# A query and key projection as three rounded products, with the context tile split by ScalarE and GpSimd

## The chip, the cores and the metric

The kernel runs on one NeuronCore of a Trainium2 chip. The metric is the device time of one execution in microseconds (us). The engines are TensorE (PE in the profile; PEld is its loading of weights), VectorE (DVE), ScalarE (ACT), GpSimd (POOL) and SyncE (SP, which here only issues transfers).

## The reference, cut to what matters

Thirty-two tiles of 128x1024 pass through four layers with a residual each: a first cross-attention, a feed-forward with signed weights, a second cross-attention and a mixture of low-rank products. The change is in the first one, with `init` the context tile:

```
q = einsum('dc,bct->btd', Wq, init) + bq          # Wq, Wk: 64 x 128, init: 128 x 1024
k = einsum('dc,bct->bdt', Wk, init) + bk
attention = softmax(einsum('btd,bds->bts', q, k))
out = einsum('bts,bsc->bct', attention, einsum('oc,bct->bto', Wv, x) + bv)
```

Everything is float32. TensorE multiplies either full float32 operands or operands rounded to a shorter form (`F32R`). Where the kernel wants nearly full accuracy at the rate of the rounded form, it splits each operand into a rounded part and a rest ("hi" and "lo") and adds three products: hi x hi, lo x hi and hi x lo.

## The kernel before

Each engine has a program written by hand, and semaphores tie them together. All five run the same loop over k (`iterations`, L633): two opening iterations, 30 in full form, two closing ones. Iteration k works on three tiles at once: it *prepares* tile b = k, *attends* with tile a = k - 1 and runs the *chain* (feed-forward, second attention, low-rank products) of tile c = k - 2. `nth(per, b, n)` is the count that a semaphore has when tile b has reached its n-th event. `half(h)` is columns 512h to 512h + 511.

The order on TensorE within one full iteration (`body`, L1195):

- eight `query_scores(a, t)` (L1141) into the two banks of `scores`, whose row maxima DVE takes (L880), with the products `keys_through_queries` (L1152 to L1155) and the first steps of the chain between them;
- the feed-forward (L1166, L1167), and `key_scores(a, s)` (L1180, L1181) for s = 0 and 1;
- a loop over s = 0 to 7: `key_scores(a, s + 2)`, then parts of the chain, then `weigh_values(a, s)` (L1192), six products that add attention times values to `acc`. `weigh_values` waits at its start for both `p_hi_ready` and `p_lo_ready` of its s;
- within s = 7 and ahead of `weigh_values(a, 7)`: the second attention's products (L1300, L1302), the query and key projection of the next tile, `wqkT` x `c_in` into `scores[0]` (L1307), column sums by `ones` (L1314), eight transposes of `c_in` (L1321), and two transposes of `den_wide` (L1325);
- after the loop: transposes of `xn_3` (L1345), the values of the next tile (L1127, called `values`), the low-rank products (L1357, L1370 to L1376). The next iteration's transposes of `xn_1` (L1207) wait for `out_ready`, which DVE's last step L1099 gives.

For each s, ACT writes `prob` as an exponential of the scores (L783) and the rounded `p_hi` (L790); DVE writes `p_lo = prob - p_hi` (L991) and from s = 1 on adds `prob` to `p_sum` (L996, L999). `prob`, `p_hi`, `p_lo` and `p_sum` are all in SBUF, so L991 and L999 read two SBUF operands. At s = 6 the DVE runs `p_lo` of 6, `p_sum` of 6, then `kwT` (L917) and a reciprocal (L1026), and at s = 7 `p_lo` of 7 (L991), `res` (L1031), statistics (L862 to L870) and the copy `den_wide` (L1038).

After the projection, ACT works without a pause through `q_hl` and `k_hh` (L812, L814, a half each), `cT_hi` (L819, L821), `xn_3` (L727, two halves) and `den_rows` (L733, two halves). DVE's L903, L904 (`x1_half`) wait for `den_rows`, and behind them on DVE stand all steps up to L1099.

GpSimd does little: `res = x1 + bias_rows` on 128x1024 once in an iteration (L705), and four times two operations on 128x1 (L696, L697, called `norm_scale`).

`oscale` is a 128x1024 tile that is also `xn_2` and `result`. `q_hl` holds the query of the tile that is attended; its last reader in an iteration is `key_scores(a, 7)`, at s = 5.

Of the kernel before, what the change touches and what calls it, by code (L numbers as in the profile page):

```python
# [18 lines left out]
F32 = mybir.dt.float32  # L19
# [29 lines left out]
def build(nc, x, ctx_, wq0, bq0, wk0, bk0, wv0, bv0, w_ffn, b_ffn, gate, ics, ocs,  # L49
# [13 lines left out]
    with top:  # L63
        def sb(name, shape, dt=F32, stack=top):
            return stack.enter_context(nc.sbuf_tensor(name, shape, dt))
# [5 lines left out]
        ident = sb("ident", [P, P])  # L71
        ones = sb("ones", [P, 32])
        minus_half = sb("minus_half", [P, 1])
        wqkT = sb("wqkT", [P, P])
        wvT = sb("wvT", [P, P])
        bqk_col = sb("bqk_col", [P, 1])
        bv_col = sb("bv_col", [P, 1])
# [45 lines left out]
        with ExitStack() as tmp:  # L123
# [65 lines left out]
            with nc.Block() as block:  # L189
# [85 lines left out]
                def _(dve):  # L275
# [45 lines left out]
                    for n, (kind, i) in enumerate(groups):  # L321
                        if kind == "sign":
                            continue
                        s = bank[n % 8]
                        dve.wait_ge(filled, n + 1)
                        if kind == "small":
                            nc.vector.tensor_copy(wqkT[:, :], s[:, 0:P])
                            last = nc.vector.tensor_copy(wvT[:, :], s[:, P:2 * P])
                        elif kind == "gate":
                            dve.wait_ge(fold_made, 6)  # L330
                            both = s[:, 0:T * 2 * E].rearrange("p (t e) -> p t e", t=T)
                            nc.vector.tensor_copy(gateT[:, :, 0:E], both[:, :, 0:E])
                            last = nc.vector.tensor_copy(lowT[:, :, HR:HR + E], both[:, :, E:2 * E])
                        elif kind == "low":
                            last = nc.vector.tensor_scalar(lowT[:, 4 * i:4 * i + 4, 0:HR],
                                                           s[:, :].rearrange("p (t e) -> p t e", t=4), LORA, None, ALU.mult)
                        elif kind == "b":
                            turned = s[:, :].rearrange("q (t p) -> q t p", t=4)
                            hi, lo = (b[:, :].rearrange("q (p t) -> q t p", t=T)[:, 4 * i:4 * i + 4, :] for b in (bT_hi, bT_lo))
                            nc.vector.tensor_copy(hi, turned).then_inc(b_hi_made, 1)  # L340
                            dve.wait_ge(b_hi_made, i + 1)
                            last = nc.vector.tensor_tensor(lo, turned, hi.bitcast(F32), ALU.subtract)
                        elif kind == "bk_col":
                            nc.vector.tensor_copy(key_bias[:, :], s[:, 0:T])
                            last = nc.vector.tensor_copy(bqbk[:, :], s[:, T:T + 1])
                        elif kind == "m":
                            dve.wait_ge(m_hi_made, i + 1)
                            if i >= STAGES:
                                dve.wait_ge(m_stored[i % STAGES], 16 * (i // STAGES))
                            last = nc.vector.tensor_tensor(m_stage[:, i % STAGES, :], s[:, :],  # L350
                                                           m_hi[:, f_order[i // 2], columns(i)].bitcast(F32), ALU.subtract)
                        else:
                            last = nc.vector.tensor_copy(query_bias[:, columns(i)], s[:, :])
                        last.then_inc(copied, 1)
# [129 lines left out]

        xnT = sb("xnT", [P, T, P])
        den_wide = xnT[:, 0:2, :].rearrange("p t c -> p (t c)")
        oscale = sb("oscale", [P, D])
        c_val = sb("c_val", [P, D])
        stat = [sb(f"stat{i}", [P, 12]) for i in range(4)]
        mean_var = [sb(f"mean_var{i}", [P, 2]) for i in range(4)]  # L490
# [17 lines left out]
        result = oscale  # L508
        attn = sb("attn", [P, P])
        gate_parts = attn  # L510
        attnT = sb("attnT", [P, P])
        low = attn
        lowT_hi = sb("lowT_hi", [P, P], F32R)
        lowT_lo = sb("lowT_lo", [P, P], F32R)

        def psum(name, shape):
            return top.enter_context(nc.psum_tensor(name, shape, F32))
# [15 lines left out]

        cT_done = sem("cT_done")
        qk_done = sem("qk_done")
        doubled = sem("doubled")
        v_done = sem("v_done")
        maxscores_done = sem("maxscores_done")
# [102 lines left out]
        with nc.Block() as block:  # L641
# [47 lines left out]
            @block.gpsimd  # L689
            def _(pool):  # L690
                def norm_scale(i, b):

                    pool.wait_ge(var_ready[i], nth(1, b, 1))
                    pool.wait_ge(normed[i], nth(2, b - 1, 2) if i == 3 else nth(1, b - 1, 1))
                    pool_norm[i].begin(b)
                    pool_norm[i].chain(pool, nc.gpsimd.tensor_tensor(rstd[i][:, :], var_eps[i][:, :], minus_half[:, :], ALU.pow))  # L696
                    nc.gpsimd.tensor_tensor(shift[i][:, :], neg_mean[i][:, :], rstd[i][:, :], ALU.mult).then_inc(shift_ready[i], 1)  # L697
                    pool_norm[i].end()

                def body(k, prepare, attend, chain):  # L700
                    b, a, c = k, k - 1, k - 2
                    if chain:
                        pool.wait_ge(x1_ready, nth(2, c, 2))
                        pool.wait_ge(out_ready, nth(2, c - 1, 2))
                        nc.gpsimd.tensor_tensor(res[:, :], x1[:, :], bias_rows[:, :], ALU.add).then_inc(biased, 1)  # L705
                    if chain:
                        norm_scale(2, c)
                    if prepare:
                        norm_scale(0, b)
                    if chain:  # L710
                        norm_scale(3, c)
                    if attend:
                        norm_scale(1, a)

                iterations(pool, body)
# [3 lines left out]
            def _(act):  # L719
# [20 lines left out]
                def body(k, prepare, attend, chain):  # L740
# [35 lines left out]
                    for s in range(T):  # L776
                        if chain and s == 1:
                            act.wait_ge(key_col_ready, nth(1, c, 1))
                        if attend:
                            act.wait_ge(scores_done, nth(8, a, s + 1))  # L780
                            act.wait_ge(p_lo_ready, nth(8, a, s - 1))
                            act.wait_ge(p_summed, nth(6, a, (0, 0, 1)[s] if s < 3 else s - 2))
                            nc.scalar.activation(prob[s % 2][:, :], scores[s % 2][:, :], ACT.Exp).then_inc(exp_ready, 1)  # L783
                        if chain and s == 4:
                            act.wait_ge(y_lo_ready, nth(2, c, 2))
                            transposed_half(2, c)
                        if attend:
                            act.wait_ge(exp_ready, nth(8, a, s + 1))
                            act.wait_ge(pv_done, nth(8, a, s - 1))
                            nc.scalar.activation(p_hi[s % 2][:, :], prob[s % 2][:, :], ACT.Identity).then_inc(p_hi_ready, 1)  # L790
                        if chain and s == 3:
                            act.wait_ge(x2_ready, nth(2, c, 2))
                            normalize(2, c, xn_2, res)
                        if chain and s == 6:

                            act_chain.begin(c)
                            act.wait_ge(s_max_ready, nth(1, c, 1))
                            act_chain.chain(act, nc.scalar.activation(r_bias[:, :], r_max[1][:, :], ACT.Identity, scale=SCALE1))
                            act_chain.end()
                            act.wait_ge(attnT_done, nth(1, c - 1, 1))  # L800
                            nc.scalar.activation(attn[:, :], shared[0][:, 0:P], ACT.Exp, bias=r_bias[:, :], scale=SCALE1,
                                                 accum_out=r_sum[1][:, :]).then_inc(attn_ready, 1)
                        if prepare and s == 6:
                            normalize(0, b, xn, xn)
                        if chain and s == 6:
                            act.wait_ge(attnT_done, nth(1, c, 1))
                            act.wait_ge(att_done, nth(2, c - 1, 2))
                            nc.scalar.activation(attnT[:, :], shared[1][:, 0:P], ACT.Identity).then_inc(attnT_ready, 1)
                    if prepare:
                        for h in range(2):  # L810
# [298 lines left out]
            def _(pe):  # L1109
# [85 lines left out]
                def body(k, prepare, attend, chain):  # L1195
# [71 lines left out]
                    for s in range(T):  # L1267
# [33 lines left out]
                            pe.wait_ge(kwT_ready, nth(2, a, 2))  # L1301
                            mm(shared[0][:, :], attnT[:, :], c_val[:, half(0)], start=True, stop=True).then_inc(att_done, 1)  # L1302
                        if prepare and s == 7:
                            pe.wait_ge(c_loaded, nth(16, b, 16))
                            pe.wait_ge(exp_ready, nth(8, a, 7))
                            for h in range(2):
                                mm(scores[0][:, half(h)], wqkT[:, :], c_in[:, half(h)], start=True, stop=True).then_inc(qk_done, 1)  # L1307
                        if attend and s == 7:

                            pe.wait_ge(p_summed, nth(6, a, 6))  # L1310
# [91 lines left out]
```

## Time and profile before

| | |
|---|---|
| median of 3 runs | 2158.94 us (2157.11 to 2161.94) |
| the profiled execution, its time | 2155.61 us |
| its span, first to last instruction | 2153.8 us |
| granted TensorE clock, mean | 0.997 of full speed |
| busy: PE, DVE, ACT, POOL | 98%, 86%, 54%, 12% |

The busy share of PE is taken from instructions that overlap, so 98% says that something was under way on it nearly always, not that it ran at its peak. Start times of consecutive instructions say more, and the sections below use them.

### The profile page before, as it was taken

The page shows a single profiled execution, that of the slowest core. Times are in us where ns is not written, and L with a number is a line of the kernel's source. Part 1 is how long each engine was busy: PE and PEld are TensorE (multiplying, and loading weights), DVE is VectorE, ACT ScalarE, POOL GpSimd, SP SyncE. Part 2 cuts the span into 40 slices and gives each one's busy share as a digit, 9 for nine tenths or more (in the row PEclk, how much of TensorE's full clock was granted, in tenths as well). Part 3 has the DMA queues.
Part 4 walks back from the last instruction along what each step waited for, and adds up shares of the span by engine and source line. Part 5 has one row for each costly group of instructions (what it writes and reads, how often), then busy time and mean ns, then how long its engine had stood idle before and what let it go on. Part 6 is the DMA issues. An engine that isn't in the chain of part 4 may idle for free.

```text
span 2153.8 us, 35686 instructions
## 1 busy us (share of the span) xinstructions
PE 2119.5 (98%) x11487; PEld 1667.0 (77%) x11487; DVE 1854.2 (86%) x3099; ACT 1155.1 (54%) x1722; POOL 260.4 (12%) x302
## 2 busy tenths in 40 slices
PE   9979999999999999999999999999999999999998
PEld 7857777778777777787777778777777787777776
DVE  8268898988888998888898988888998888898984
ACT  4145555655555565555555655555565555555652
POOL 0001111111101110111111111101110111111100
PEclk9999999999999999999999999999999999999999
DMA  6354343333343323334343333343323334343310
GB/s 217 142 156 127 118 132 102 95 119 126 127 134 119 117 90 105 127 127 136 117 130 103 95 119 125 128 134 120 117 89 106 127 127 136 117 129 104 93 54 30
DMA packets 110874, 254.03 MB, mean 118 GB/s; under 512 B 12976, under 2 KB 14272, under 8 KB 110848
## 3 DMA queue, kind: packets, MB, share of 16 engines
q1 hardware_dynamic: 110848, 253.69, 36.3%
q8 instruction: 16, 0.26, 0.0%
q14 instruction: 10, 0.08, 0.0%
HBM read 215.89 MB, written 20.97 MB: 110 GB/s over the span
## 4 chain that ended last, share of the span: by engine, by line
PE 84%; DVE 6%; issue 3%; ACT 1%; DVEq 0%; POOL 0%; POOLq 0%; ACTq 0%
PE acc L1192 17%; PE shared L1121 7%; PE shared L1166 6%; PE shared L1167 6%; PE scores L1181 5%; PE scores L1180 5%; PE acc L1152 4%; PE scores L1141 4%; PE acc L1155 4%; PE acc L1153 4%; PE shared L1357 3%; PE shared L1284 3%; PE scores L1127 2%; PE scores L1307 2%; DVE neg_max L880 2%
## 5 line engine op out<-in xcount | busy, mean ns | idle before, releaser
L991 DVE TENSOR_TENSOR p_lo<-prob,p_hi 128x1024 fp32r<-128x1024 f32 x256 | 312.2, 1219 | 103.6 <-ACT p_hi L790 85.7
L783 ACT ACTIVATE prob<-scores 128x1024 f32<-128x1024 f32 x256 | 260.8, 1019 | 241.1 <-PE scores L1181 189.9
L880 DVE TENSOR_REDUCE neg_max<-scores 128x1 f32<-128x1024 f32 x256 | 309.4, 1220 | 44.8 <-PE scores L1141 42.1
L696 POOL TENSOR_TENSOR rstd<-var_eps,minus_half 128x1 f32<-128x1 f32 x128 | 126.2, 986 | 1746.1 <-DVE var_eps L870 1746.1
L790 ACT ACTIVATE p_hi<-prob 128x1024 fp32r<-128x1024 f32 x256 | 271.3, 1060 | 42.7 <-PE acc L1192 38.5
L1152 PE MATMUL acc<-m_hi,cT_hi 128*128 128x512 f32 x512 | 218.3, 426 | 3.6 <-DVE cT_lo L1052 2.7
L1166 PE MATMUL shared<-signT,y_hi 128*128 128x512 f32 x512 | 205.5, 401 | 0.0
L1155 PE MATMUL acc<-m_ring,cT_hi 128*128 128x512 f32 x512 | 203.3, 397 | 0.0
L1153 PE MATMUL acc<-m_hi,cT_lo 128*128 128x512 f32 x512 | 203.1, 397 | 0.0
L1180 PE MATMUL scores<-q_hl,k_hh 128*128 128x512 f32 x512 | 201.0, 392 | 1.8 <-DVE q_m L973 1.4
L1181 PE MATMUL scores<-q_m,k_l 128*128 128x512 f32 x512 | 202.0, 395 | 0.0
L1167 PE MATMUL shared<-signT,y_lo 128*128 128x512 f32 x512 | 200.9, 392 | 0.0
L999 DVE TENSOR_TENSOR p_sum<-p_sum,prob 128x1024 f32<-128x1024 f32 x160 | 194.8, 1218 | 0.0
L1192 PE MATMUL acc<-p_hi,v_hi 128*128 128x512 f32 x512 | 171.3, 416 | 4.4 <-DVE p_lo L991 3.9
L1141 PE MATMUL scores<-k_hh,q_hl 128*128 128x512 f32 x512 | 163.2, 400 | 1.8 <-DVE k_l L856 1.5
L1192 PE MATMUL acc<-p_hi,v_lo 128*128 128x512 f32 x512 | 161.3, 396 | 0.0
L1192 PE MATMUL acc<-p_lo,v_hi 128*128 128x512 f32 x512 | 160.6, 395 | 0.0
L1152 PEld LDWEIGHTS acc<-m_hi,cT_hi 128*128 128x128 f32 x512 | 96.8, 189 | 28.1 <-issue 9.0
L1180 PEld LDWEIGHTS scores<-q_hl,k_hh 128*128 128x128 f32 x512 | 96.2, 188 | 25.4 <-DVE q_m L973 1.6
L1155 PEld LDWEIGHTS acc<-m_ring,cT_hi 128*128 128x128 f32 x512 | 96.6, 189 | 23.0
L1192 PEld LDWEIGHTS acc<-p_lo,v_hi 128*128 128x128 f32 x512 | 96.0, 188 | 23.7
L1181 PEld LDWEIGHTS scores<-q_m,k_l 128*128 128x128 f32 x512 | 96.1, 188 | 23.0
(219 smaller groups left out, 4201.5 us busy)
## 6 DMA issues: line engine op xcount, KB each, us to landing
m_ring<-m_low SPq DMA_DIRECT2D x512, 256.0 KB, 3.2
c_in<-in_ctx SPq DMA_DIRECT2D x32, 512.0 KB, 3.3
xn<-in_x SPq DMA_DIRECT2D x32, 512.0 KB, 4.2
x<-in_x SPq DMA_DIRECT2D x32, 512.0 KB, 3.2
c_val<-in_ctx SPq DMA_DIRECT2D x32, 512.0 KB, 3.7
out_x<-oscale SPq DMA_DIRECT2D x32, 512.0 KB, 3.0
q_m<-q_hl SPq DMA_DIRECT2D x32, 256.0 KB, 3.1
k_hh<-k_hh SPq DMA_DIRECT2D x32, 256.0 KB, 3.5
```

The source lines that it names most:

```text
L783: nc.scalar.activation(prob[s % 2][:, :], scores[s % 2][:, :], ACT.Exp).then_inc(exp_ready, 1)
L790: nc.scalar.activation(p_hi[s % 2][:, :], prob[s % 2][:, :], ACT.Identity).then_inc(p_hi_ready, 1)
L880: nc.vector.tensor_reduce(neg_max[:, t:t + 1], scores[t % 2][:, :], AX_X, ALU.max, negate=True).then_inc(row_max, 1)
L991: nc.vector.tensor_tensor(p_lo[s % 2][:, :], prob[s % 2][:, :], p_hi[s % 2][:, :].bitcast(F32), ALU.subtract).then_inc(p_lo_ready, 1)
L1152: mm(acc[:, half(h)], cT_hi[:, f, :], m_hi[:, f, half(h)], start=f == 0, stop=False)
L1153: mm(acc[:, half(h)], cT_lo[:, f, :], m_hi[:, f, half(h)], start=False, stop=False)
L1155: mm(acc[:, half(h)], cT_hi[:, f, :], m_ring[:, u % SLOTS, :], start=False, stop=f == T - 1).then_inc(kw_unit_done, 1)
L1166: mm(shared[h][:, :], y_hi[:, f, :], signT[:, f, half(h)], start=f == 0, stop=False)
L1167: last = mm(shared[h][:, :], y_lo[:, f, :], signT[:, f, half(h)], start=False, stop=f == T - 1)
L1180: mm(scores[s % 2][:, half(h)], k_hh[:, s * P:(s + 1) * P], q_hl[:, half(h)], start=True, stop=False)
L1181: last = mm(scores[s % 2][:, half(h)], k_l1[:, s * P:(s + 1) * P], q_m[:, half(h)], start=False, stop=True)
L1192: last = mm(acc[:, half(h)], v[:, s, :], p[s % 2][:, half(h)], start=first, stop=end)
```

## The change

The stationary operand `wqkT` becomes `wqk_hi` and `wqk_lo`, both made in the setup by DVE. The moving operand `c_in` is split in every iteration: ACT writes `c_hi` at s = 4, after `p_hi` of 4, and GpSimd writes `c_lo = c_in - c_hi`, behind `norm_scale(0, b)` in its program and once `scores_done` says that `key_scores(a, 7)` is over. `c_hi` lies in the memory of `oscale`, `c_lo` in that of `q_hl`; `attnT` shares its memory with `lowT_lo`. The two products of L1307 become six: for each half hi x hi and lo x hi, then a wait for `c_lo_ready`, then hi x lo for each half. `qk_done` comes with these last two.

```diff
-        wqkT = sb("wqkT", [P, P])
+        wqk_hi = sb("wqk_hi", [P, P], F32R)
+        wqk_lo = sb("wqk_lo", [P, P], F32R)
...
-                            nc.vector.tensor_copy(wqkT[:, :], s[:, 0:P])
-                            last = nc.vector.tensor_copy(wvT[:, :], s[:, P:2 * P])
+                            nc.vector.tensor_copy(wqk_hi[:, :], s[:, 0:P]).then_inc(b_hi_made, 1)
+                            nc.vector.tensor_copy(wvT[:, :], s[:, P:2 * P])
+                            dve.wait_ge(b_hi_made, 1)
+                            last = nc.vector.tensor_tensor(wqk_lo[:, :], s[:, 0:P], wqk_hi[:, :].bitcast(F32), ALU.subtract)
...
-        oscale = sb("oscale", [P, D])
+        with ExitStack() as before:
+            oscale = sb("oscale", [P, D], F32, before)
+        c_hi = sb("c_hi", [P, D], F32R)
+        c_lo = q_hl
...
-        attnT = sb("attnT", [P, P])
+        with ExitStack() as before:
+            attnT = sb("attnT", [P, P], F32, before)
         low = attn
+        lowT_lo = sb("lowT_lo", [P, P], F32R)
         lowT_hi = sb("lowT_hi", [P, P], F32R)
-        lowT_lo = sb("lowT_lo", [P, P], F32R)
...
                     if prepare:
                         norm_scale(0, b)
+                        pool.wait_ge(c_hi_ready, nth(1, b, 1))
+                        pool.wait_ge(scores_done, nth(8, a, 8))
+                        nc.gpsimd.tensor_tensor(c_lo[:, :], c_in[:, :], c_hi[:, :].bitcast(F32), ALU.subtract).then_inc(c_lo_ready, 1)
                     if chain:
                         norm_scale(3, c)
...
+                        if prepare and s == 4:
+                            act.wait_ge(c_loaded, nth(16, b, 16))
+                            act.wait_ge(xnT_done[2], nth(2, c, 2))
+                            nc.scalar.activation(c_hi[:, :], c_in[:, :], ACT.Identity).then_inc(c_hi_ready, 1)
...
                             act.wait_ge(att_done, nth(2, c - 1, 2))
+                            act.wait_ge(out_done, nth(2, c - 1, 2))
                             nc.scalar.activation(attnT[:, :], shared[1][:, 0:P], ACT.Identity).then_inc(attnT_ready, 1)
...
                         if prepare and s == 7:
-                            pe.wait_ge(c_loaded, nth(16, b, 16))
+                            pe.wait_ge(c_hi_ready, nth(1, b, 1))
                             pe.wait_ge(exp_ready, nth(8, a, 7))
                             for h in range(2):
-                                mm(scores[0][:, half(h)], wqkT[:, :], c_in[:, half(h)], start=True, stop=True).then_inc(qk_done, 1)
+                                mm(scores[0][:, half(h)], wqk_hi[:, :], c_hi[:, half(h)], start=True, stop=False)
+                                mm(scores[0][:, half(h)], wqk_lo[:, :], c_hi[:, half(h)], start=False, stop=False)
+                            pe.wait_ge(c_lo_ready, nth(1, b, 1))
+                            for h in range(2):
+                                mm(scores[0][:, half(h)], wqk_hi[:, :], c_lo[:, half(h)], start=False, stop=True).then_inc(qk_done, 1)
```

## Rows read from the trace of the kernel before

**Rows 1.** The page: busy time of the engines, and the chain that ended last.

```profile
PE 2119.5 (98%) x11487; PEld 1667.0 (77%) x11487; DVE 1854.2 (86%) x3099; ACT 1155.1 (54%) x1722; POOL 260.4 (12%) x302
...
PE 84%; DVE 6%; issue 3%; ACT 1%; DVEq 0%; POOL 0%; POOLq 0%; ACTq 0%
```

**Rows 2.** Timeline of PE, 1023 to 1054 us: start, length, engine, line, instruction.

```profile
1023.56 0.71 PE L1192 MATMUL acc<-p_hi,v_hi 128*128 128x512 f32 x2
1024.11 0.63 PE L1192 MATMUL acc<-p_hi,v_lo 128*128 128x512 f32 x2
1024.57 0.63 PE L1192 MATMUL acc<-p_lo,v_hi 128*128 128x512 f32 x2
...
1030.50 0.39 PE L1181 MATMUL scores<-q_m,k_l 128*128 128x512 f32 x1
...
1032.85 0.70 PE L1192 MATMUL acc<-p_hi,v_hi 128*128 128x512 f32 x2
...
1036.04 1.88 PE L1307 MATMUL scores<-c_in,wqkT 128*128 128x512 f32 x4
1037.85 0.64 PE L1314 MATMUL scores<-p_sum,ones 128*32 128x256 f32 x8
...
1039.85 0.44 PE L1325 MATMUL scores<-ident,xnT 128*128 128x128 f32 x2
...
1053.04 1.25 PE L1121 MATMUL shared<-ident,p_sum 128*128 128x128 f32 x8
```

**Rows 3.** Timeline of ACT in the same iteration; in brackets its idle time and releaser.

```profile
1024.90 1.02 ACT L783 ACTIVATE prob<-scores 128x1024 f32<-128x1024 f32 x1
...
1028.53 1.03 ACT L783 ACTIVATE prob<-scores 128x1024 f32<-128x1024 f32 x1 [1.52 <-DVE p_sum L999]
...
1037.10 0.68 ACT L812 ACTIVATE q_hl<-scores,bqk_col 64x512 fp32r<-64x512 f32 x1 [2.09 <-PE scores L1307]
...
1042.47 1.06 ACT L733 ACTIVATE prob<-scores 128x512 f32<-128x512 f32 x2
```

**Rows 4.** Timeline of POOL in the same iteration.

```profile
1019.06 1.46 POOL L696 TENSOR_TENSOR rstd<-var_eps,minus_half 128x1 f32<-128x1 f32 x1 [25.15 <-DVE var_eps L870]
...
1039.54 0.55 POOL L696 TENSOR_TENSOR rstd<-var_eps,minus_half 128x1 f32<-128x1 f32 x1 [11.00 <-DVE var_eps L870]
...
1053.66 2.39 POOL L705 TENSOR_TENSOR res<-x,bias_rows 128x1024 f32<-128x1024 f32 x1 [3.99 <-DVE oscale L1099]
```

**Rows 5.** Groups by line and form, whole span: count, busy us, mean ns.

```profile
L696 POOL TENSOR_TENSOR rstd<-var_eps,minus_half 128x1 f32<-128x1 f32 x128 | 126.2, 986 | 1746.1 <-DVE var_eps L870 1746.1
```

**Rows 6.** Timeline of DVE in the same iteration.

```profile
1018.89 1.22 DVE L991 TENSOR_TENSOR p_lo<-prob,p_hi 128x1024 fp32r<-128x1024 f32 x1
1020.03 1.22 DVE L999 TENSOR_TENSOR p_sum<-p_sum,prob 128x1024 f32<-128x1024 f32 x1
...
1030.35 1.22 DVE L999 TENSOR_TENSOR p_sum<-p_sum,prob 128x1024 f32<-128x1024 f32 x1
1031.48 1.22 DVE L991 TENSOR_TENSOR p_lo<-prob,p_hi 128x1024 fp32r<-128x1024 f32 x1
...
1035.10 1.22 DVE L991 TENSOR_TENSOR p_lo<-prob,p_hi 128x1024 fp32r<-128x1024 f32 x1 [0.59 <-DVE r_inv L1026]
...
1039.38 0.42 DVE L1038 COPY xnT<-scores 128x256 f32<-128x256 f32 x1
...
1043.15 0.69 DVE L903 TENSOR_TENSOR prob<-acc,prob 128x512 f32<-128x512 f32 x1 [0.24 <-ACT prob L733]
...
1052.18 1.40 DVE L1099 SCALAR_TENSOR_TENSOR oscale<-shared,r_inv,res 128x512 f32<-128x512 f32 x2
```

**Rows 7.** Busy us by window, second opening iteration: PE, PEld, DVE, ACT, POOL; clock.

```profile
152.00:156.00 4.00, 2.52 (x10) 1.49 (x9) 1.86 (x2) 3.94 (x4) 0.00 (x0) 1.00 0.00 0
```

**Rows 8.** Timeline of all engines, first iteration, 117 to 120 us.

```profile
117.83 0.19 POOL L697 TENSOR_TENSOR shift<-neg_mean,rstd 128x1 f32<-128x1 f32 x1
...
119.21 0.67 ACT L812 ACTIVATE q_hl<-scores,bqk_col 64x512 fp32r<-64x512 f32 x1
```

More of the change, by code:

```diff
@@ L340, in _ @@
                             nc.vector.tensor_copy(hi, turned).then_inc(b_hi_made, 1)
-                            dve.wait_ge(b_hi_made, i + 1)
+                            dve.wait_ge(b_hi_made, i + 2)
                             last = nc.vector.tensor_tensor(lo, turned, hi.bitcast(F32), ALU.subtract)
@@ L535, in build @@
         qk_done = sem("qk_done")
+        c_hi_ready = sem("c_hi_ready")
+        c_lo_ready = sem("c_lo_ready")
         doubled = sem("doubled")
```

## The prediction

> **What bounds the kernel now.** I read the page first: something is under way on PE for 98% of the span, and the chain that ended last is PE for 84% and DVE for 6% [rows 1]. So PE's time counts one for one, as long as nothing else is as late. Whether something is, only the timelines of one full iteration can say. In PE's timeline [rows 2] look at starts. Six rounded 512-column products of L1192 start 0.23 us apart (0.46 for two, 1024.11 to 1024.57). The first two take 0.55, because transposes of full float32 stand ahead of them: a change of format costs 0.09. The projection to be replaced fills 1036.04 to 1037.85, 1.81 us.
>
> Then I looked for the places at which PE is only just not late. There are three.
>
> - `weigh_values(a, 6)` starts at 1032.85 [rows 2] and needs `p_lo` of 6, which DVE finishes at 1031.48 + 1.22 = 1032.70 [rows 6]. Slack: about 0.1.
> - The transposes L1325 start at 1039.85 [rows 2]; DVE's copy `den_wide` ends at 1039.80 [rows 6]. Slack: none, PE waits there.
> - The transposes of `xn_1` start at 1053.04 [rows 2] and need the first half of L1099, 1052.18 + 0.70 = 1052.88 [rows 6]. Slack: 0.1.
>
> DVE is thus as late as PE from s = 6 to the start of the next iteration. Over the same stretch ACT runs without a pause from L812 at 1037.10 to L733 at 1042.47 [rows 3], and DVE's L903 waits 0.24 for it [rows 6].
>
> **Part by part.** *The products.* Removed: 1.81 us. Added: six rounded products, 6 x 0.23 = 1.39, and one change of format ahead of them, 0.09: 1.48, or 1.57 if there is another one behind. PE itself gains 0.24 to 0.33 in each of 32 iterations, 8 to 10 us. But L1325 stands 2 us behind and waits for `den_wide`, whose time hangs on `p_lo` of 7 and DVE's own steps, not on the projection. I count the gain as 0 and keep 0.33 as the bound.
>
> *The order of the halves.* Before, the first `qk_done` came with the first half: ACT's L812 started 1.06 after the projection did [rows 2, 3], 0.86 for the half and 0.20 behind it. Now the first half ends with the fifth of six products: 0.09 + 5 x 0.23 + 0.20 = 1.45 us. ACT's unbroken run starts 0.39 later, L903 waits 0.39 longer, and everything behind it on DVE up to L1099 moves with it. With 0.1 of slack that is 0.3 per iteration at 1053.04. Bounds: 0, if some step in between has slack that I don't see, and 0.39.
>
> *`c_hi` on ACT.* It is like L783 and L790, 1.0 us, and goes in ahead of the L783 at 1024.90 [rows 3]. The next L783 waits 1.52 us for DVE's `p_sum` [rows 3], which swallows it; `p_lo` of 5, which stands one 1.14 us pitch of DVE ahead of the L999 at 1030.35 [rows 6], needs its `p_hi` only at 1029.2. I count 0. Without that cover it would be 1.0. Its waits (`c_loaded`, whose load is issued after the feed-forward, and the transposes of `xn_2`) are over by then. The new wait ahead of `attnT` is for the previous iteration's last products: 0.
>
> *`c_lo` on GpSimd.* Nearest row: L705, the same shape and number of operands, 2.39 us [rows 4]. It waits for `key_scores(a, 7)`, whose last product starts at 1030.50 and is over by about 1030.9 [rows 2]. PE needs `c_lo` at 1036.04 + 0.09 + 4 x 0.23 = 1037.05. By itself it has 6 us for 2.4, and the GpSimd work behind it, `norm_scale(3, c)`, comes at 1039.54 [rows 4]. Taken alone it costs nothing.
>
> But it doesn't run alone. GpSimd's L696 takes 0.55 us at 1039.54 and 1.46 us at 1019.06 [rows 4]. In the second case DVE is in L991, an operation with two operands in SBUF, and then in L999, another one [rows 6]. The mean of 986 ns over 128 [rows 5] is 0.55 for 67 of them and 1.46 for 61: two in each iteration, every time. GpSimd is held while such a DVE instruction reads. And it is let in when that one is over: L696 ends at 1020.52, 0.49 after L999 has started at 1020.03, though L999 is followed by more of its kind. So the two engines take turns by whole instructions, and GpSimd gets its turn between two DVE instructions that stand back to back. L696 reads one element, so its turn costs DVE nothing visible. `c_lo` reads 1024 elements twice: 2.39 less the 0.19 of a tiny operation [rows 8] is 2.2 us.
>
> The Trainium skill says the same of the port (SBUF — State Buffer, "Who interferes with whom"): a DVE instruction with two SBUF inputs contends with a GpSimd instruction that reads SBUF, and the second to issue is blocked until the first is over, not slowed. This case's trace shows the half in which GpSimd is blocked (1.46 against 0.55); the half in which DVE is blocked no row of before shows.
>
> Where `c_lo` falls decides. It asks at 1030.95, while DVE is in L999 (1030.35 to 1031.48) [rows 6]. Its turn comes at 1031.48, and there stands `p_lo` of 6, the one with 0.1 of slack. Held for 2.2 us, it ends at 1034.90, and `weigh_values(a, 6)` starts at 1035.0 in place of 1032.85: 2.15 us late. Behind it, DVE's `p_sum` of 6, `kwT` and `p_lo` of 7 come late too (the last by 1.6, since 0.59 of idle time [rows 6] is used up), no later than PE's own 2.15. Nothing gives the time back, for PE is busy for the rest of the iteration. Bounds for the hold: 0 (DVE isn't blocked by GpSimd) and 2.39.
>
> Would the gap cost clock as well? In 152 to 156 us PE is busy for 2.52 of 4 us and the granted clock is 1.00 [rows 7]. I count nothing.
>
> *First iteration.* `c_lo` comes after `norm_scale(0, 0)`, at 118.0 [rows 8], and ends at 120.4; the last products and 0.3 behind them give ACT's L812 at 120.9 in place of 119.2: 1.7 us once.
>
> *The setup.* One more 128x128 operation of DVE, some tenths of a us, with PE busy on the next groups: 0. No DMA is moved; SP's queue waits for nothing new.
>
> **The sum.** 31 iterations attend and prepare: 31 x (2.15 + 0.3) = 76, and 1.7 for the first: 78 us. On the profiled execution's 2155.6 that is 2233; it ran 3.3 under the median of 2158.9, so on that 2236. With the bounds of the small terms (PE's 0.33 kept; 0.39 in full and 2.39 for the hold) this case has 2214 to 2246.
>
> **The rivals.**
>
> - *GpSimd loses the turn as long as DVE has instructions with two SBUF operands back to back.* Then `c_lo` starts when `kwT` does, two pitches of 1.14 behind 1031.48, at 1033.76, is over at about 1036.0, and holds `p_lo` of 7 (1035.10) for 0.9 us. `den_wide` and L1325 come 0.9 later: 31 x 0.9, 28 us, 2187. For: DVE is in a row there. Against: L696 got in at 1020.03. Chance 0.10.
> - *DVE isn't held, but the later half counts.* 31 x 0.3 + 1.7 = 11 us, 2170. For: no row shows DVE held; L999 at 1020.03 keeps its 1.22 us though L696 had its turn there [rows 6]. Against: only that it would be one-sided. Chance 0.10.
> - *DVE isn't held, and the two small terms cancel*: within 0.2%, 2155 to 2163. Chance 0.06.
> - *Faster.* GpSimd takes the port in pieces too short to delay `p_lo` of 6 by more than its 0.1, `c_lo` is there by 1037.05, and the iteration is paced by PE's work alone, so that DVE's and ACT's waits shift with it: 32 x 0.3, some 10 us less, 2149. It decides from the point at which `p_lo` of 6 is less than 0.1 late. For: PE at 98%. Against: L1325 and L903 wait already. Chance 0.10.
> - The forecast, DVE held at `p_lo` of 6: 0.64.
>
> **How the numbers follow.** The time is the likeliest case's, 2236. The range goes down to 2165, which leaves out the last two cases whole, takes in the case of 2187 and most of that of 2170, and up to 2246. About 0.2% is what a measurement of this kernel can tell from no change. Slower: 0.64 + 0.10 + 0.10 = 0.84; same 0.06; faster 0.10.
>
> **What the changed kernel's profile would show.** `c_lo` on POOL with over 2.4 us, from about 1030.9 of such an iteration; `p_lo` of 6 on DVE 2.2 us late or that much longer, with an idle PE ahead of an L1192 for 2 us in every iteration, its releaser `p_lo`; the six products in 1.5 us; ACT's L812 1.45 after their start; L1325 still behind `den_wide`; the clock still at 1.00. I am wrong if L991 keeps its 1.22 us and its start beside `c_lo`, or if `c_lo` comes at another point of DVE's row, where more slack stands.

## The result

The changed kernel takes 2245.39 us in the median of 4 runs (2243.78 to 2247.48), the kernel before 2158.03 (4 runs, 2154.97 to 2161.94): 1.040 times as long, 95% interval 1.0389 to 1.0415. That is 87 us more; 2236 was forecast, with a range of 2165 to 2246.

### The profile page after: what moved, and what is told of

Read it like the earlier page. It is cut to its first block, busy times and chain, and to the rows that moved or that the text cites. A ratio compares the mean times of both kernels' runs of the same rounds, so it can differ in the third digit from the quotient of the medians.

```text
span 2245.7 us, 35943 instructions
## 1 busy us (share of the span) xinstructions
PE 2135.3 (95%) x11551; PEld 1685.2 (75%) x11551; DVE 1921.3 (86%) x3100; ACT 1184.9 (53%) x1754; POOL 351.9 (16%) x334
## 4 chain that ended last, share of the span: by engine, by line
PE 70%; ACT 9%; DVE 8%; issue 7%; DVEq 0%; ACTq 0%; POOL 0%; POOLq 0%
PE acc L1209 12%; PE shared L1183 5%; PE shared L1138 5%; PE shared L1184 5%; PE scores L1198 5%; PE scores L1197 4%; PE acc L1169 4%; PE scores L1158 4%; PE acc L1172 4%; PE acc L1170 4%; PE shared L1378 3%; PE scores L1144 2%; PE shared L1301 2%; DVE neg_max L897 2%; DVE xnT L977 2%
## 5 line engine op out<-in xcount | busy, mean ns | idle before, releaser
L1008 DVE TENSOR_TENSOR p_lo<-prob,p_hi 128x1024 fp32r<-128x1024 f32 x256 | 380.3, 1485 | 87.0 <-ACT p_hi L802 85.7
L705 POOL TENSOR_TENSOR rstd<-var_eps,minus_half 128x1 f32<-128x1 f32 x128 | 127.0, 992 | 1671.6 <-DVE var_eps L887 1671.6
L1209 PE MATMUL acc<-p_hi,v_hi 128*128 128x512 f32 x512 | 174.2, 422 | 72.5 <-ACT p_hi L802 64.9
L1209 PE MATMUL acc<-p_hi,v_lo 128*128 128x512 f32 x512 | 163.6, 401 | 0.0
L1209 PE MATMUL acc<-p_lo,v_hi 128*128 128x512 f32 x512 | 163.3, 400 | 0.0
L1209 PEld LDWEIGHTS acc<-p_hi,v_hi 128*128 128x128 f32 x512 | 87.4, 192 | 92.2 <-ACT p_hi L802 76.2
L829 ACT ACTIVATE q_hl<-scores,bqk_col 64x512 fp32r<-64x512 f32 x64 | 43.7, 682 | 156.3 <-PE scores L1328 155.5
L1209 PEld LDWEIGHTS acc<-p_lo,v_hi 128*128 128x128 f32 x512 | 97.7, 191 | 24.1
L1209 PEld LDWEIGHTS acc<-p_hi,v_lo 128*128 128x128 f32 x512 | 97.9, 191 | 23.3
```

The costliest lines, as they stand in the source:

```text
L1008: nc.vector.tensor_tensor(p_lo[s % 2][:, :], prob[s % 2][:, :], p_hi[s % 2][:, :].bitcast(F32), ALU.subtract).then_inc(p_lo_ready, 1)
L1209: last = mm(acc[:, half(h)], v[:, s, :], p[s % 2][:, half(h)], start=first, stop=end)
```

## The profile after

The page of the changed kernel: its span, busy time, chain, and three groups (count, busy us, mean ns, then idle time ahead and who ended it). L1008 is the old L991 (`p_lo`), L1209 the old L1192 (`weigh_values`).

```profile
span 2245.7 us, 35943 instructions
...
PE 2135.3 (95%) x11551; PEld 1685.2 (75%) x11551; DVE 1921.3 (86%) x3100; ACT 1184.9 (53%) x1754; POOL 351.9 (16%) x334
...
PE 70%; ACT 9%; DVE 8%; issue 7%; DVEq 0%; ACTq 0%; POOL 0%; POOLq 0%
...
L1008 DVE TENSOR_TENSOR p_lo<-prob,p_hi 128x1024 fp32r<-128x1024 f32 x256 | 380.3, 1485 | 87.0 <-ACT p_hi L802 85.7
...
L1209 PE MATMUL acc<-p_hi,v_hi 128*128 128x512 f32 x512 | 174.2, 422 | 72.5 <-ACT p_hi L802 64.9
```

Against [rows 1], PE has 95% in place of 98% and the chain is PE for 70%, not 84%. The same 256 instructions `p_lo` take 68 us more than before (380.3 against 312.2), and 31 x 2.2 is 68: one long one in each of 31 iterations. `weigh_values` has 72 us of idle time ahead of it.

One iteration of it, GpSimd first. `q_hl<-c_in,c_hi` is `c_lo`.

```profile
1012.62 2.84 POOL L721 TENSOR_TENSOR q_hl<-c_in,c_hi 128x1024 fp32r<-128x1024 f32 x1 [2.43 <-PE scores L1198]
```

DVE at the same time (for [rows 6]):

```profile
1011.99 1.22 DVE L1016 TENSOR_TENSOR p_sum<-p_sum,prob 128x1024 f32<-128x1024 f32 x1
1013.13 3.41 DVE L1008 TENSOR_TENSOR p_lo<-prob,p_hi 128x1024 fp32r<-128x1024 f32 x1
1016.46 1.21 DVE L1016 TENSOR_TENSOR p_sum<-p_sum,prob 128x1024 f32<-128x1024 f32 x1
...
1018.38 1.22 DVE L1008 TENSOR_TENSOR p_lo<-prob,p_hi 128x1024 fp32r<-128x1024 f32 x1
...
1022.66 0.42 DVE L1055 COPY xnT<-scores 128x256 f32<-128x256 f32 x1
...
1027.27 0.69 DVE L920 TENSOR_TENSOR prob<-acc,prob 128x512 f32<-128x512 f32 x1 [1.08 <-ACT prob L745]
```

PE (for [rows 2]):

```profile
1013.89 0.60 PE L1138 MATMUL shared<-ident,x 128*128 128x128 f32 x4
1016.69 0.70 PE L1209 MATMUL acc<-p_hi,v_hi 128*128 128x512 f32 x2 [2.20 <-ACT p_hi L802]
...
1020.10 0.40 PE L1325 MATMUL scores<-c_hi,wqk_lo 128*128 128x512 f32 x1
...
1021.35 0.64 PE L1335 MATMUL scores<-p_sum,ones 128*32 128x256 f32 x8
...
1023.29 0.38 PE L1346 MATMUL scores<-ident,xnT 128*128 128x128 f32 x2
...
1026.11 1.36 PE L1138 MATMUL shared<-ident,p_sum 128*128 128x128 f32 x8 [0.17 <-ACT p_sum L739]
```

`c_lo` asks at 1012.62, in the middle of `p_sum`. It takes 2.84 us: the 2.39 of [rows 4] and nearly 0.5 until its turn behind `p_sum`. DVE's next instruction, `p_lo` of 6, starts on time at 1013.13 and lasts 3.41 us in place of 1.22: the hold of 2.2 us shows in the length, not in an idle time. It is over at 1016.54, and `weigh_values(a, 6)` starts 0.15 later, as it did before. PE's gap is 2.20 us. The profile names `p_hi` as its releaser, because an instruction of that name ends nearby; it is `p_hi` of 7. The count that PE waits for is that of 6, which is over long before. Where a releaser looks odd, compare the counts of the waits in the code with the ends of the instructions.

The starts of the residual sum (the old L705), one in each iteration, give the iteration: 62.13 us before, 64.57 now. But seven of the 30 full ones take 1.5 us more than that. This is one of them, by windows (us, then busy us and count of PE, PEld, DVE, ACT, POOL, then the granted clock, the DMA engines' share and GB/s), and its gap on PE's timeline:

```profile
944.00:948.00 4.00, 4.00 (x21) 3.24 (x20) 4.00 (x6) 3.33 (x6) 1.56 (x2) 1.00 0.00 0
948.00:952.00 4.00, 1.79 (x8) 1.37 (x6) 4.00 (x3) 2.57 (x4) 1.42 (x1) 0.80 0.40 131
952.00:956.00 4.00, 4.00 (x11) 2.46 (x10) 2.77 (x5) 0.00 (x0) 0.00 (x0) 0.77 0.00 0
```

```profile
950.65:953.35 2.70, 2.70 (x6) 2.13 (x7) 2.67 (x4) 0.00 (x0) 0.00 (x0) 0.50 0.19 74
```

```profile
950.65 1.19 PE L1209 MATMUL acc<-p_hi,v_hi 128*128 128x512 f32 x2 [2.21 <-ACT p_hi L802]
...
953.35 1.27 PE L1317 MATMUL shared<-c_val,attnT 128*128 128x512 f32 x2
```

Behind the gap the clock is at half, the lower of its two levels (1.2 of 2.4 GHz): the six products of `weigh_values` take 2.70 us (950.65 to 953.35) against 1.47 in the iteration above. So the 92 us by which the span grew are 30 x 2.43 = 73 for the longer iteration, 7 x 1.5 = 10.5 for the clock, and 8.5 in the opening.

## The experiments

Each run is told with its iteration, read from the starts of the same GpSimd instruction, beside its time (the median). The ratio is to runs of the kernel before taken beside it, with its 95% interval in brackets.

**Is it the hold, or the new products?** Two runs take the change apart. The first drops GpSimd's subtraction; its third product reads `c_hi`, so the term with `c_lo` is wrong.

```diff
-                        nc.gpsimd.tensor_tensor(c_lo[:, :], c_in[:, :], c_hi[:, :].bitcast(F32), ALU.subtract)...
...
-                                mm(scores[0][:, half(h)], wqk_hi[:, :], c_lo[:, half(h)], start=False, stop=True)...
+                                mm(scores[0][:, half(h)], wqk_hi[:, :], c_hi[:, half(h)], start=False, stop=True)...
```

> The changed kernel without GpSimd's c_lo: the third product of each half reads c_hi in place of c_lo, so the query and key are wrong by the missing term, and six products stand as before. Theory (GpSimd's read holds DVE's p_lo of 6): iteration back from 64.57 to 62.1 to 62.5 us, time 2158 to 2170, all L991-like p_lo at 1.22. Rival (the six products, c_hi on ACT or the new waits cost it): iteration stays above 64, time above 2230.

Measured: 2166.5 us, ratio 1.0037 (1.0025 to 1.0048), iteration 62.37. The six products, `c_hi` and the waits cost 0.24 per iteration and no more.

The second adds only a GpSimd subtraction to the kernel before, with a wait on ACT so that its output isn't overwritten too early.

```diff
+                        pool.wait_ge(c_loaded, nth(16, b, 16))
+                        pool.wait_ge(scores_done, nth(8, a, 8))
+                        nc.gpsimd.tensor_tensor(q_hl[:, :], c_in[:, :], bias_rows[:, :], ALU.subtract).then_inc(c_lo_ready, 1)
...
+                            act.wait_ge(c_lo_ready, nth(1, b, 1))
```

> The kernel before with one GpSimd subtraction of 128x1024 (c_in minus bias_rows into q_hl) at the place and with the waits of c_lo; products, ACT and order as before. Theory: the whole hold without the rest, 2.1 to 2.2 us in each of 31 iterations, 2224 to 2238 with some loss of clock. Rival (GpSimd alone harmless): 2158.

Measured: 2242.4 us, ratio 1.0391 (1.0374 to 1.0409). GpSimd and DVE in its timelines:

```profile
1007.03 2.81 POOL L713 TENSOR_TENSOR q_hl<-c_in,bias_rows 128x1024 fp32r<-128x1024 f32 x1 [2.43 <-PE scores L1186]
```

```profile
1007.54 3.39 DVE L996 TENSOR_TENSOR p_lo<-prob,p_hi 128x1024 fp32r<-128x1024 f32 x1
```

The iteration is 64.26, 2.13 more, and twelve of the 30 take 1.6 more still, for the clock. This passes the upper end of what was expected, 2238: the clock costs 19 us in these twelve, and the opening is 5 us longer. An instruction whose result nobody uses gives nearly the whole loss.

**Reads or any access?** GpSimd writes zeros to `c_lo` in place of the subtraction, so the term with `c_lo` is left out.

```diff
+        pad = sb("pad", [P, 1])
...
-                        nc.gpsimd.tensor_tensor(c_lo[:, :], c_in[:, :], c_hi[:, :].bitcast(F32), ALU.subtract).then_inc(c_lo_ready, 1)
+                        nc.gpsimd.tensor_tensor(pad[:, :], minus_half[:, :], minus_half[:, :], ALU.subtract)
+                        nc.gpsimd.memset(c_lo[:, :].bitcast(F32), 0.0).then_inc(c_lo_ready, 1)
```

> The changed kernel with GpSimd's subtraction replaced by a memset of c_lo to 0 at the same place, behind one 128x1 operation that carries the waits, so the third term is left out. GpSimd writes as many bytes and reads none. Theory in its narrow form (DVE's second SBUF operand meets GpSimd's reads): p_lo of 6 at 1.22 and the time of the run without the split. Wider form (any GpSimd access to SBUF holds DVE): p_lo of 6 longer by the memset's own length, some 1 us, and the time between.

Measured: 2167.5 us, ratio 1.0044 (1.003 to 1.0058), iteration 62.37, the same as without a split. In its timelines the memset (0.96 us) stands beside `p_lo` of 6:

```profile
1038.76 0.96 POOL L723 MEMSET q_hl<- 128x1024 f32 x1
```

```profile
1038.68 1.22 DVE L1010 TENSOR_TENSOR p_lo<-prob,p_hi 128x1024 fp32r<-128x1024 f32 x1
```

None of the 256 `p_lo` of this run and none of its `p_sum` is longer than 1.23. Writing 128x1024 holds nothing; what the memset lacks is the reads (and the subtraction itself, which these runs can't tell from them).

**The order of the products.**

```diff
                             for h in range(2):
                                 mm(... wqk_hi[:, :], c_hi[:, half(h)], start=True, stop=False)
                                 mm(... wqk_lo[:, :], c_hi[:, half(h)], start=False, stop=False)
-                            pe.wait_ge(c_lo_ready, nth(1, b, 1))
-                            for h in range(2):
+                                pe.wait_ge(c_lo_ready, nth(1, b, 1))
                                 mm(... wqk_hi[:, :], c_lo[:, half(h)], start=False, stop=True).then_inc(qk_done, 1)
```

> The changed kernel with its six products ordered half by half: the first qk_done comes behind the third product, 0.98 us after the start, not behind the fifth at 1.45. Theory of the order: the pause ahead of L903's group on DVE and PE's waits behind it shrink by 0.2 to 0.5 in each iteration, 2230 to 2239. Rival (ACT's later start is harmless): 2245.

Measured: 2244.6 us, ratio 1.0402 (1.0384 to 1.0419): no gain in time. Yet the iteration fell from 64.57 to 64.09, by 0.48 where 0.2 to 0.5 was expected. Of the 30 full iterations fifteen, not seven, now take some 1.5 more, and the mean clock is 0.983 in place of 0.988. Both theories of the order failed as put. The time is the rival's, 2245, but by chance: ACT's start does count, and the clock ate what it gave.

The same order without the split (third product reads `c_hi`, the term is wrong):

> As the run without a split (third product reads c_hi, GpSimd's c_lo left out), with the six products half by half. It shows the change with the split for nothing. Theory (PE's 0.33 is lost behind den_wide, and the late qk_done made the 0.24 of the run without a split): iteration 62.1, time 2155 to 2160, no difference from before. Rival (PE paces): 62.13 less 0.33, time 2147.

Measured (11 runs): 2155.7 us, ratio 0.9995 (0.9986 to 1.0004), iteration 62.13, to the hundredth that of before. Its transposes of `den_wide` (the old L1325):

```profile
1043.55 0.44 PE L1341 MATMUL scores<-ident,xnT 128*128 128x128 f32 x2 [0.23 <-DVE xnT L1052]
```

So the 0.24 of the run without a split was the late `qk_done`, and of the 0.33 that PE gains, 0.23 shows as a wait for DVE two steps on. With the split for nothing, the change would be worth nothing.

**The clock.** Twenty dummy transposes into `scores[0]`, free at that point, fill PE's gap:

```diff
+                        if prepare and attend and s == 6:
+                            pe.wait_ge(exp_ready, nth(8, a, 7))
+                            for i in range(20):
+                                nc.tensor.transpose(scores[0][:, 0:P], ident[:, :], ident[:, :])
```

> The changed kernel with 20 dummy transposes on PE in the 2.2 us gap ahead of weigh_values of 6 (20 x 0.106 = 2.1 us). The hold stays. Theory: the seven iterations of 66.05 us become 64.57 like the others, since PE no longer pauses and its clock isn't lowered, 10 us less, 2233 to 2238. Rival (the longer iterations have another cause): 2245, seven long iterations still there.

Measured: 2234.8 us, ratio 1.0361 (1.0343 to 1.0378), 10.6 less than the changed kernel; mean clock 0.995. `p_lo` of 6 is still at 3.45 in the mean, every iteration from the third on is 64.56 to 64.64, and none is long. The transposes in the gap of one iteration, and the start of `weigh_values(a, 6)` behind them:

```profile
1007.25 2.35 PE L1317 MATMUL scores<-ident 128*128 128x128 f32 x20
1009.65 0.70 PE L1209 MATMUL acc<-p_hi,v_hi 128*128 128x512 f32 x2
```

The hold is as before and only the pause of PE is gone, so it was the pause that cost the clock.

**The place of the hold.** `c_lo` also waits for `p_sum` of 6:

```diff
                         pool.wait_ge(scores_done, nth(8, a, 8))
+                        pool.wait_ge(p_summed, nth(6, a, 6))
```

> The changed kernel with GpSimd's c_lo also waiting for p_sum of 6, so that it starts beside kwT and the reciprocal and meets p_lo of 7, not of 6. Theory of the hold: p_lo of 6 at 1.22, p_lo of 7 (0.59 of idle time ahead of it) starts or ends about 0.9 late, iteration 62.9 to 63.2 us, time 2180 to 2192. Rival (the cost is the GpSimd operation itself, wherever it stands): 2245.

Measured: 2192.8 us, ratio 1.0169 (1.0152 to 1.0186), iteration 63.19. GpSimd and DVE:

```profile
1052.03 2.37 POOL L722 TENSOR_TENSOR q_hl<-c_in,c_hi 128x1024 fp32r<-128x1024 f32 x1 [5.37 <-DVE p_sum L1017]
```

```profile
1053.22 2.27 DVE L1009 TENSOR_TENSOR p_lo<-prob,p_hi 128x1024 fp32r<-128x1024 f32 x1 [0.60 <-DVE r_inv L1044]
```

GpSimd now starts first and isn't held (2.37, as [rows 4]); `p_lo` of 7 waits 1.05 for the rest of it, a little more than the 0.9 expected, and the time is 0.8 us past the range. The same instruction costs 1.06 per iteration in place of 2.44. PE pauses for 1.06 us in this iteration, ahead of the transposes of `den_wide`, and none of the 30 is long.

**DVE does it itself**, ahead of `p_lo` of 7, products by halves:

```diff
-                        nc.gpsimd.tensor_tensor(c_lo[:, :], c_in[:, :], c_hi[:, :].bitcast(F32), ALU.subtract).then_inc(c_lo_ready, 1)
...
+                        if prepare and s == 6:
+                            dve.wait_ge(c_hi_ready, nth(1, b, 1))
+                            dve.wait_ge(scores_done, nth(8, a, 8))
+                            nc.vector.tensor_tensor(c_lo[:, :], c_in[:, :], c_hi[:, :].bitcast(F32), ALU.subtract).then_inc(c_lo_ready, 1)
```

> No split on GpSimd: DVE makes c_lo itself ahead of p_lo of 7 (1.14 us of which 0.59 fall in its idle time), products by halves. Theory: DVE paces this stretch, so 1.14 less 0.59 is 0.55 per iteration, 62.5 to 62.8 us, time 2170 to 2182: the slow place is cheaper on the busiest engine than on the idle one. Rival (DVE isn't as late as PE there): 2150 to 2160.

Measured: 2182.3 us, ratio 1.0117 (1.01 to 1.0134), iteration 62.88. It costs 0.75 and not 0.55, just past both expected ranges, since 0.19 of idle time stays ahead of it:

```profile
1047.62 1.22 DVE L1044 TENSOR_TENSOR q_hl<-c_in,c_hi 128x1024 fp32r<-128x1024 f32 x1 [0.19 <-DVE r_inv L1040]
```

The busiest of the helpers does the work more cheaply than the idle one does in one piece.

**Two pieces.** `c_lo` in halves, behind `p_sum` of 6 and behind `p_lo` of 7, the last product behind the column sums:

```diff
+                        pool.wait_ge(p_summed, nth(6, a, 6))
+                        nc.gpsimd.tensor_tensor(c_lo[:, half(0)], c_in[:, half(0)], c_hi[:, half(0)].bitcast(F32), ALU.subtract)...
+                        pool.wait_ge(p_lo_ready, nth(8, a, 8))
+                        nc.gpsimd.tensor_tensor(c_lo[:, half(1)], c_in[:, half(1)], c_hi[:, half(1)].bitcast(F32), ALU.subtract)...
...
```

> GpSimd makes c_lo in two halves, one behind p_sum of 6 (beside kwT, the reciprocal and the idle time of DVE), one behind p_lo of 7, where DVE has only one SBUF operand; the last product comes behind the column sums. Theory: neither half meets a DVE instruction with two SBUF operands for more than 0.1 us, iteration 62.1 to 62.4, time 2157 to 2168. Rival (any GpSimd work of 2.4 us costs): above 2200.

Measured: 2167.9 us, ratio 1.0052 (1.0035 to 1.0068), iteration 62.39. GpSimd's halves in one iteration:

```profile
1041.98 1.27 POOL L722 TENSOR_TENSOR q_hl<-c_in,c_hi 128x512 fp32r<-128x512 f32 x1 [5.37 <-DVE p_sum L1019]
1044.47 1.30 POOL L724 TENSOR_TENSOR q_hl<-c_in,c_hi 128x512 fp32r<-128x512 f32 x1 [1.21 <-DVE p_lo L1011]
```

Of the 256 `p_lo`, 253 are at 1.22. All of GpSimd's work is there, and it costs 0.26 per iteration. The run without a split, whose first `qk_done` also comes behind the fifth product, cost 0.24.

**Towards a version that beats both.** DVE is as late as PE in this stretch, so its chain has to start earlier. On ACT the normalisation of `xn` moves behind `p_hi` of 7, and the exponential of 7 ahead of `attnT`. First in the kernel before:

```diff
                             nc.scalar.activation(prob[s % 2][:, :], scores[s % 2][:, :], ACT.Exp).then_inc(exp_ready, 1)
+                        if chain and s == 7:
+                            ...                                 # the three lines of attnT, from s == 6
...
-                        if prepare and s == 6:
-                            normalize(0, b, xn, xn)
...
+                    if prepare:
+                        normalize(0, b, xn, xn)
```

> The kernel before with two moves on ACT: the normalisation of xn goes behind p_hi of 7, and the exponential of 7 goes ahead of attnT. p_lo of 7 should start up to 0.59 us earlier. Theory that DVE is as late as PE from there on: little gain by itself, since PE's own work is as long, 2150 to 2158. Rival (DVE alone paces): 2140.

Measured (11 runs): 2155.4 us, ratio 0.9991 (0.9982 to 1.0001), iteration 62.07. The move by itself is not told from nothing. Then with the change, `c_lo` in two halves behind `p_lo` of 7:

> The changed kernel with the same two moves on ACT, GpSimd's c_lo in two halves behind p_lo of 7, and the last product behind the column sums. Theory: no hold, DVE's chain 0.59 earlier, so that PE's 0.33 counts: iteration 61.7 to 61.9, time 2143 to 2150, faster than both kernels. Rival (the 0.33 is lost all the same): as the reordered kernel before, or 0.3 per iteration behind it.

Measured: 2179.4 us, ratio 1.0103 (1.0087 to 1.0119), iteration 62.80: a miss. There is no hold, but `c_lo` is late. `p_lo` of 7 and, behind it, DVE's wait for ACT; the first half of `c_lo`; and, on ACT, the first `q_hl`:

```profile
1047.11 1.23 DVE L1010 TENSOR_TENSOR p_lo<-prob,p_hi 128x1024 fp32r<-128x1024 f32 x1
...
1056.44 0.69 DVE L922 TENSOR_TENSOR prob<-acc,prob 128x512 f32<-128x512 f32 x1 [1.23 <-ACT prob L747]
```

```profile
1048.47 1.30 POOL L722 TENSOR_TENSOR q_hl<-c_in,c_hi 128x512 fp32r<-128x512 f32 x1 [7.37 <-DVE p_lo L1010]
```

```profile
1050.38 0.68 ACT L831 ACTIVATE q_hl<-scores,bqk_col 64x512 fp32r<-64x512 f32 x1 [2.95 <-PE scores L1329]
```

`q_hl` comes 3.3 us behind the start of `p_lo` of 7 (1047.11), against 2.0 before [rows 3, 6], and DVE waits 1.23 for ACT behind it. Part of that is only `p_lo` of 7 being early. Measured from the start of the projection (0.86 behind the product of L1321 at 1047.75), `q_hl` comes 1.77 later, against 1.06 before. Of these 0.7, 0.39 is the order of the products, as counted in the prediction, and 0.3 is PE's wait for the first half of `c_lo`: its product starts at 1049.83, 0.53 behind the one ahead of it in place of 0.23.

```profile
1047.75 1.02 PE L1321 MATMUL shared<-c_val,attnT 128*128 128x512 f32 x2
...
1049.30 0.40 PE L1327 MATMUL scores<-c_hi,wqk_lo 128*128 128x512 f32 x1
1049.83 0.50 PE L1329 MATMUL scores<-q_hl,wqk_hi 128*128 128x512 f32 x1
```

The 0.7 is also what the iteration grew by against the reordered kernel before (62.80 less 62.07). So the last run uses every pause of DVE between operations with two SBUF operands, with `c_lo` in the memory of `xnT`, and strict halves:

```diff
+                        pool.wait_ge(sc1_done, nth(1, c, 1))
+                        for cols, semaphore, count in ((slice(0, 256), p_summed, nth(6, a, 4)), (slice(256, 512), p_summed, nth(6, a, 6)),
+                                                       (slice(512, 1024), p_lo_ready, nth(8, a, 8))):
+                            pool.wait_ge(semaphore, count)
+                            nc.gpsimd.tensor_tensor(c_lo[:, cols], c_in[:, cols], c_hi[:, cols].bitcast(F32), ALU.subtract).then_inc(c_lo_ready, 1)
...
```

> As the reordered changed kernel, but products strictly by halves and GpSimd's c_lo (now in the memory of xnT) in three pieces at DVE's pauses from operations with two SBUF operands: 256 columns behind p_sum of 4, 256 behind p_sum of 6, 512 behind p_lo of 7. Theory: holds of at most 0.1 us, the first qk_done early, DVE's chain up to 0.5 earlier, so that PE's 0.33 counts in part: iteration 61.8 to 62.1 us, time 2146 to 2157. Rival (0.2 to 0.3 of hold in two of the pieces, or a pace set elsewhere): 62.1 to 62.5, 2157 to 2170.

Measured (11 runs): 2152.5 us, ratio 0.9975 (0.9966 to 0.9984), iteration 61.90. GpSimd's pieces, and DVE's operations with two SBUF operands around them:

```profile
1029.64 0.74 POOL L725 TENSOR_TENSOR c_lo<-c_in,c_hi 128x256 fp32r<-128x256 f32 x1
1034.98 0.74 POOL L725 TENSOR_TENSOR c_lo<-c_in,c_hi 128x256 fp32r<-128x256 f32 x1 [4.60 <-DVE p_sum L1020]
1036.91 1.30 POOL L725 TENSOR_TENSOR c_lo<-c_in,c_hi 128x512 fp32r<-128x512 f32 x1 [1.19 <-DVE p_lo L1012]
```

```profile
1030.28 1.22 DVE L1012 TENSOR_TENSOR p_lo<-prob,p_hi 128x1024 fp32r<-128x1024 f32 x1
...
1035.61 1.23 DVE L1012 TENSOR_TENSOR p_lo<-prob,p_hi 128x1024 fp32r<-128x1024 f32 x1
```

No piece and no `p_lo` is stretched here; in the whole trace 254 of 256 `p_lo` are at 1.22, the other two at 1.4 and 1.5. It is faster than both kernels: 0.25% under the kernel before and 93 us under the changed one, with the same products and the same split. Of the 0.23 by which the iteration is shorter than before, 0.06 came with the move on ACT alone; which of the other edits gives the rest isn't shown.

## Why the prediction was right

- *The contention with GpSimd, from L696's 1.46 against 0.55.* Right, mechanism and place. The hold was put at 2.2 us; DVE's `p_lo` of 6 shows 3.41 less 1.22. The step that no row of before could show, that DVE is held in its turn, is shown by the subtraction alone and by the memset. All 31 such `p_lo` of the trace are held, and no other. The Trainium skill (SBUF — State Buffer, "Who interferes with whom") has both halves: the second to issue is blocked, and a GpSimd instruction that only writes does not contend with a DVE instruction of this kind. The traces agree, 3.39 with a reading instruction and 1.22 with a writing one.
- *The turn at the boundary.* Right: GpSimd asked in the middle of `p_sum` and had its turn behind it, ahead of a DVE instruction that was ready.
- *PE's lateness at `weigh_values(a, 6)`*, forecast 2.15: a gap of 2.20.
- *PE's 0.33 counted as 0.* Right in the sum. The run by halves without a split has the iteration of before. In the changed kernel itself the place was another: `den_wide` ends at 1023.08 and L1346 starts at 1023.29, so PE doesn't wait there, since DVE had made up 0.59 of the hold. It is given back behind, where ACT is late for the transposes of `xn_3` (0.17) and DVE waits for ACT at L920 (1.08).
- *The order of the halves*, forecast 0.3 per iteration: 0.24 without the hold (62.37 less 62.13), 0.48 beside it (64.57 less 64.09). The hold alone is 2.13 per iteration in the kernel before, and 1.96 between the two runs by halves (64.09 less 62.13). The two terms don't simply add up, though their sum came out.
- *The sum per iteration*, 2.45: measured 2.43.
- *The clock.* Here the working was wrong: "I count nothing", and the sign "the clock still at 1.00" did not come. It is the largest term missed, 10 us, shown by filling the gap. The row that I read, 2.52 us busy of 4 at a clock of 1.00 [rows 7], had gaps of 0.23 and 1.25 us, not one of 2.2. It couldn't speak for one twice as long.
- *The opening*, forecast 1.7 for the first iteration and 2.45 for the second: 8.5. Without a split it is already 3.9 longer than before (the first residual sum starts at 184.5 in that run and at 180.6 in the kernel before). About 1.5 of this is there at the start of the first iteration. The opening also differs by a microsecond or two between kernels whose setup is the same (182.0 in the reordered form of the kernel before, whose edit doesn't touch the setup). `c_lo` of the first iteration adds 2.0 (ACT's first `q_hl` at 122.70, against 120.71 without a split), near the 1.7. The remaining 2.6 is the second iteration's hold and some clock; I have not taken it apart further. The clock is 0.62 and 0.52 over 120 to 124 and 124 to 128 us, against 1.00 and 0.62 in the kernel before.
- *The range.* The measured 2245.39 lies 0.6 us below its upper end, and that it still lies inside is luck. The upper end was made of 0.39 for the halves and 2.39 for the hold, and the iteration needed neither: 2.43 was measured. What filled the room was the clock and the opening, counted as 0 and as 4. The profiled execution, 2247.48, lies above it. The lower end, 2214, is worked out from the profiled 2155.6; from 2158.9, on which 2236 stands, it is 2217.

## What to carry to other kernels

An engine that is idle for 88% of the span is not free: before giving GpSimd a subtraction that reads SBUF, lay its window over DVE's timeline and mark the DVE instructions with two SBUF operands; the hold falls on the one behind the boundary, and its price is the length of the hold less that instruction's slack. If the slack is too small, cut the operation into pieces and tie each to the end of such a DVE instruction behind which DVE does something else. And when a change speeds up an engine that is 98% busy, look for the next wait behind it: two steps on, another engine may be just as late.

## What was not expected of the hardware

A pause of 2.2 us on PE brought the granted clock down in some iterations and not in others: seven of 30 at an iteration of 64.57, twelve at 64.26, fifteen at 64.09, at quite regular distances, at 1.5 to 1.6 us each. The 30 iterations do the same work, so I take it that the moment at which the pause falls decides which is hit; no run tests this. An edit that shortens the iteration can so lose its gain to the clock, as the order by halves did. What sets the distances stays open.

A held DVE instruction shows no idle time and starts on schedule; it is only longer (3.41 against 1.22). The view of waits doesn't name it. The longest duration of a line, beside its median (3420 against 1220 ns for L1008), finds it at once.
